# Silu attention: one silu instruction for both units of a group in place of one per unit

## The chip, the cores and the metric

The kernel runs on one core of one Trainium2 chip. The core has a matrix engine (TensorE, PE in the profile; PEld is its loading of weights), a vector engine (VectorE, DVE), an activation engine (ScalarE, ACT), a general engine (GpSimd, POOL) and a queue for transfers (SyncE, SP). Each engine runs its own instructions in the order of the program; between engines semaphores are counted up and waited for. The metric is device time in microseconds (us) of one execution.

## The reference, cut to what matters

Six layers run one after the other on 64 images of 1024 positions and 32 channels. The third is the one that the change touches:

```python
q = silu(x @ Wq + bq); k = silu(x @ Wk + bk); v = silu(x @ Wv + bv); u = x @ Wu + bu
scores = einsum('bhnd,bhmd->bhnm', qh, kh) / sqrt(hd)            # 4 heads of 8
scores = where(causal, scores * scores, 0.0)
self_attn = einsum('bhnm,bhmd->bhnd', silu(scores), vh)
# beside it pos_attn from a table of relative positions, a layer norm, a gate with u, a projection
```

There is no softmax: each score is squared, masked, put through silu, and the weights so made multiply v.

## The kernel before, in words

The layer is `silu_attention_layer`. One image at a time is in the middle of the work; a *stage* of the pipeline (`body`, run for each image by `over_stages`, 12 stages to one turn of a loop) also prepares the two images behind it and finishes the two ahead of it. The attention of an image is cut into 12 groups, `GROUPS_B`: a pair (qc, kb) of one half of the queries and one block of 128 keys. A group has two *units*, one for each pair of heads, so a stage has 24 units, n = 0 to 23. A unit's tile has 128 partitions (keys) and 2 x m columns (two heads, m queries), where m is 512, 384, 256 or 128, by how much of the triangle is left.

A unit goes through these steps:

- PE, `scores` (L890): two matmuls into `p_s[n % 2]`. There are two such tiles, so scores of unit n wait until unit n-2 has been read from its tile.
- The square. For 16 units ACT reads the scores and writes the squares, `square_scores` (L819), into the ring `sq` of 8 units. For the other 8 (`ON_DVE`: n = 0, 1, 6, 7, 12, 13, 18, 19) DVE reads and masks them, `read_scores` (L1037), and POOL squares them in SBUF (L739). Eight of ACT's units lie on the diagonal and are masked afterwards by POOL's `select` (L745).
- ACT, `weigh` (L830): silu of the squares into the ring `wt` of 8 units, `LAG` = 5 units behind the scores.
- PE, `add_up` (L903): for each group, at odd n, the eight matmuls of both units with v into `p_o`; four units further back.

PE's and ACT's orders are written out by hand: for each n, ACT squares unit n (if it is its own) and then weighs unit n-5; PE computes the scores of n, then one piece of the other images' work (`M_PLACE`: transposes of k, q, o; projections; positions; the output L984), then, at odd n, an `add_up`. In what follows S(n) is the scores of unit n on PE, sq(n) the square on ACT, W(n) the silu of unit n. All of them use semaphores: `scored`, `act_squared`, `dve_read`, `weighed` (counted once per unit), `summed` (once per group).

```python
if n >= 2:
    semaphore, value = scores_read(o, n - 2)   # PE: the tile's last reader, ACT or DVE
    pe.wait_ge(semaphore, value)
```

The page of the profile names the tiles with a letter for each layer: `b_` is this one.

Of the kernel before, what the change touches and what calls it, by code (L numbers as in the profile page):

```python
# [8 lines left out]
ACT = mybir.ActivationFunctionType  # L9
# [395 lines left out]
def wait(eng, semaphore, value):  # L405

    if not isinstance(value, int) or value > 0:
        eng.wait_ge(semaphore, value)
# [66 lines left out]
def over_stages(eng, body):  # L475

    for w in range(B_FIRST, B_LOOPED):
        body(Stage(w))
    with eng.Fori(0, (B - 2 - B_LOOPED) // B_UNROLL) as k:
        for d in range(B_UNROLL):  # L480
            body(Stage(B_LOOPED + d, k))
    for w in range(B - 2, B_LAST + 1):
        body(Stage(w))
# [121 lines left out]
def silu_attention_layer(nc, t, kept):  # L605
# [3 lines left out]
    with ExitStack() as ctx:  # L609
        def sb(name, shape, dt=F32):  # L610
            return ctx.enter_context(nc.sbuf_tensor("b_" + name, shape, dt))
# [4 lines left out]
        def sem(name):  # L616
            return ctx.enter_context(nc.semaphore("b_" + name))

        SQ_RING, RING, LAG = 8, 8, 5
# [20 lines left out]
        sq = sb("sq", [P, SQ_RING, 2, HALF])  # L640
        wt = sb("wt", [P, RING, 2, HALF])
# [18 lines left out]
        NG = len(GROUPS_B)  # L660
        UNITS = [(qc, kb, g) for qc, kb in GROUPS_B for g in range(2)]
        N = len(UNITS)
# [4 lines left out]
        def span(n):  # L667

            qc, kb, _ = UNITS[n]
            q0 = max(qc * HALF, kb * P)  # L670
            return q0, (qc + 1) * HALF - q0
# [14 lines left out]
        pool_squared, selected, weighed, summed = (  # L686
            sem("pool_squared"), sem("selected"), sem("weighed"), sem("summed"))
# [18 lines left out]
        @block.sync  # L706
        def _(sp):
            sp.dma_start(x_in[:, 0, :, :], image(src, 0)).then_inc(x_loaded[0], 16)

            def store(i):  # L710
                sp.wait_ge(result_made, i + 1)
                sp.dma_start(image(dst, i), result[:, :, :]).then_inc(stored, 16)

            def body(st):
                if "prep" in st.on:
                    q = st.image("prep")
                    if st.ref > B_FIRST:
                        wait(sp, base_made, q - 1)
                        sp.dma_start(x_in[:, st.place("prep", 2), :, :], image(src, q)).then_inc(x_loaded[st.place("prep", 2)], 16)
                if "past" in st.on:  # L720
                    store(st.image("past"))

            over_stages(sp, body)
            sp.wait_ge(stored, 16 * B)
# [83 lines left out]
        @block.scalar  # L808
        def _(act):
            act.preload_act_table(ACT.Silu)  # L810

            def body(st):
                q, nx, o, p = st.image("prep"), st.image("next"), st.image("own"), st.image("prev")

                def square_scores(n):
                    act.wait_ge(scored, 2 * N * o + 2 * (n + 1))
                    wait(act, weighed, N * o + (n + 1 - SQ_RING))
                    m = span(n)[1]
                    act.activation(sq[:, n % SQ_RING, :, 0:m], p_s[n % 2][:, :, 0:m], ACT.Square).then_inc(act_squared, 1)  # L819

                def weigh(i, n):
                    if n in ON_DVE:
                        act.wait_ge(pool_squared, len(ON_DVE) * i + (ON_DVE.index(n) + 1))
                    elif n in SELECTED:
                        act.wait_ge(selected, len(SELECTED) * i + (SELECTED.index(n) + 1))
                    else:
                        act.wait_ge(act_squared, len(ON_ACT) * i + (ON_ACT.index(n) + 1))
                    wait(act, summed, NG * i + (n // 2 + 1 - RING // 2))
                    m = span(n)[1]
                    act.activation(wt[:, n % RING, :, 0:m], sq[:, n % SQ_RING, :, 0:m], ACT.Silu,  # L830
                                   scale=1.0 / D).then_inc(weighed, 1)

                def silu_qkv(a):
                    act.wait_ge(m_made, st.made(f"qkv{a}"))
                    act.activation(qkv[:, st.place("prep", 2), :, 4 * a:4 * a + 4, :].rearrange("p k r c -> p r k c"),
                                   p_m[st.bank(f"qkv{a}")][:, 0:4 * 3 * C].rearrange("p (r k c) -> p r k c", k=3, c=C),
                                   ACT.Silu).then_inc(qkv_made, 1)

                for n in range(N):
                    if "own" in st.on and n in ON_ACT:  # L840
                        square_scores(n)
                    if "own" in st.on and n >= LAG:
                        weigh(o, n - LAG)
                    if "prev" in st.on and n < LAG:
                        weigh(p, N + n - LAG)
                    if "prep" in st.on and n in (13, 14):
                        silu_qkv(n - 13)

            over_stages(act, body)

        @block.tensor
        def _(pe):
# [5 lines left out]
            def body(st):  # L858
                q, nx, o, p = st.image("prep"), st.image("next"), st.image("own"), st.image("prev")
# [33 lines left out]
                def add_up(i, place, a):  # L893

                    qc, kb = GROUPS_B[a]
                    q0, m = span(2 * a)
                    if a == FIRST_OF[qc]:
                        wait(pe, o_copied, 2 * i - 1 + qc)
                    if a == 0:
                        pe.wait_ge(v_made, i + 1)  # L900
                    pe.wait_ge(weighed, N * i + (2 * a + 2))
                    for h in range(H):
                        ins = pe.matmul(p_o[qc][32 * h:32 * h + 32, q0 - qc * HALF:q0 - qc * HALF + m],  # L903
                                        v_pad[:, place, kb, h, :], wt[:, (2 * a + h // 2) % RING, h % 2, 0:m],
                                        start=(a == FIRST_OF[qc]), stop=(a == LAST_OF[qc]), tile_position=(0, 32 * h),
                                        skip_group_check=True)
                    ins.then_inc(summed, 1)
# [81 lines left out]
                for n in range(N):  # L989
                    if "own" in st.on:  # L990
                        scores(n)
                    for name in M_PLACE.get(n, ()):
                        if name in ("k0", "k1", "q0", "q1") and "next" in st.on:
                            turn_parts(name)
                        elif name in ("o0", "o1") and "prev" in st.on:
                            turn_o(int(name[1]))
                        elif name == "xlT" and "prep" in st.on:
                            turn_xl()
                        elif name in ("qkv0", "qkv1") and "prep" in st.on:
                            project_qkv(int(name[-1]))  # L1000
                        elif name[:3] == "pos" and "next" in st.on:
                            positions(int(name[-1]))
                        elif name == "nT" and "prev" in st.on:
                            turn_normed()
                        elif name == "uT" and "prev" in st.on:
                            project_u()
                        elif name == "out" and "past" in st.on:
                            project_out()
                    if n % 2:
                        a = (n - LAG - 4) // 2  # L1010
                        if a >= 0 and "own" in st.on:
                            add_up(o, st.place("own", 3), a)
                        if a < 0 and "prev" in st.on:
                            add_up(p, st.place("prev", 3), NG + a)
# [4 lines left out]
        def _(dve):  # L1019
# [5 lines left out]
            def body(st):  # L1025
                q, nx, o, p = st.image("prep"), st.image("next"), st.image("own"), st.image("prev")
# [5 lines left out]

                def read_scores(n):
                    dve.wait_ge(scored, 2 * N * o + 2 * (n + 1))
                    wait(dve, weighed, N * o + (n + 1 - SQ_RING))
                    m = span(n)[1]
                    dve.tensor_tensor(sq[:, n % SQ_RING, :, 0:m], p_s[n % 2][:, :, 0:m],  # L1037
                                      tri[:, 0:m].rearrange("p (r m) -> p r m", r=1).broadcast_to([P, 2, m]),
                                      ALU.mult).then_inc(dve_read, 1)
# [105 lines left out]
                for n in range(N):  # L1145
                    if "own" in st.on and n in ON_DVE:
                        read_scores(n)
# [506 lines left out]
RING = 8  # L1654
# [914 lines left out]
```

## Time and profile before

| | |
|---|---|
| time, median of 3 runs | 6068.95 us (6066.87 to 6073.85) |
| span of the profiled execution | 6064.5 us (of that execution nothing beside the span is given; the median is 4.45 us above it) |
| busy over the whole span | PE 89%, DVE 81%, ACT 79%, POOL 52% |
| this layer in steady state (441.31 to 2379.44 us, 60 stages) | PE 1805.26 us, ACT 1760.66, POOL 1476.09, DVE 1353.97 of 1938.13 |
| L830, the silu of this layer | 1440 instructions there, 1162.19 us busy |
| one undisturbed stage | 31.31 to 31.39 us |

A stage's length is read between two starts of the line L1099, which each stage has once on DVE. Busy times count an instruction from its start to its end; on ACT an instruction begins up to 0.1 us before the end of the one ahead, so sums of durations can be above the busy time. In the timeline a row is one instruction or several alike in a row (x2, x8), and the bracket at its end is the engine's idle time just before, with what ended it.

### The profile page before, as it was taken

The page shows a single profiled execution, that of the slowest core. Times are in us where ns is not written, and L with a number is a line of the kernel's source. Part 1 is how long each engine was busy: PE and PEld are TensorE (multiplying, and loading weights), DVE is VectorE, ACT ScalarE, POOL GpSimd, SP SyncE. Part 2 cuts the span into 40 slices and gives each one's busy share as a digit, 9 for nine tenths or more (in the row PEclk, how much of TensorE's full clock was granted, in tenths as well). Part 3 has the DMA queues.
Part 4 walks back from the last instruction along what each step waited for, and adds up shares of the span by engine and source line. Part 5 has one row for each costly group of instructions (what it writes and reads, how often), then busy time and mean ns, then how long its engine had stood idle before and what let it go on. Part 6 is the DMA issues. An engine that isn't in the chain of part 4 may idle for free.

```text
span 6064.5 us, 145558 instructions
## 1 busy us (share of the span) xinstructions
PE 5411.5 (89%) x43064; PEld 2287.0 (38%) x43064; DVE 4920.5 (81%) x9311; ACT 4808.2 (79%) x8146; POOL 3146.1 (52%) x3711
## 2 busy tenths in 40 slices
PE   6679999999999999468999999999999999999997
PEld 5234444444444444352333333333333333333332
DVE  7857667667677676658999999999999999999995
ACT  1159989999899899315888888888888888888887
POOL 1147777777777777632444444444444444444443
PEclk9889999999999999777999999999999999999999
DMA  3010000000000000230000000000000000000000
GB/s 114 22 48 10 9 11 10 9 10 10 9 10 10 9 10 8 63 115 7 9 9 9 9 10 9 9 9 10 10 9 9 10 9 9 9 10 9 9 8 5
DMA packets 400111, 104.64 MB, mean 17 GB/s; under 512 B 348547, under 2 KB 398676, under 8 KB 398804
## 3 DMA queue, kind: packets, MB, share of 16 engines
q1 hardware_dynamic: 398163, 94.72, 7.2%
q8 instruction: 409, 6.70, 0.5%
q14 instruction: 387, 3.16, 0.2%
q10 hardware_dynamic: 1152, 0.05, 0.0%
HBM read 61.17 MB, written 33.56 MB: 16 GB/s over the span
## 4 chain that ended last, share of the span: by engine, by line
PE 25%; DVE 17%; issue 7%; POOL 3%; ACT 2%; DVEq 1%; ACTq 0%; POOLq 0%
DVE d_peaks L2355 13%; PE d_p_o L2193 8%; PE d_p_s L2180 5%; PE d_p_k L2205 4%; PE d_p_s L2293 2%; POOL d_rstd L1989 2%; PE d_p_s L2168 2%; ACT d_wt L2077 2%; PE d_p_s L2251 1%; PE d_p_s L2233 1%; PE d_p_s L2242 1%; DVE d_squares L2373 1%; DVE d_total L2365 1%; POOL d_xl L1993 1%; ACT d_answers L2073 1%
## 5 line engine op out<-in xcount | busy, mean ns | idle before, releaser
L2355 DVE TENSOR_REDUCE d_peaks<-d_p_k 128x1 f32<-128x512 f32 x4096 | 2576.9, 681 | 203.4 <-PE d_p_k L2205 167.9
L2077 ACT ACTIVATE d_wt<-d_p_s 128x512 f32<-128x512 f32 x4096 | 2214.7, 616 | 333.2 <-PE d_p_s L2180 326.7
L2205 PE MATMUL d_p_k<-d_kT,d_qT 64*128 64x512 bf16 x4096 | 1320.6, 387 | 122.4 <-DVE d_peaks L2355 118.9
L2180 PE MATMUL d_p_s<-d_qT,d_kT 64*128 64x512 bf16 x4096 | 1339.7, 384 | 11.3 <-issue 10.8
L830 ACT ACTIVATE b_wt<-b_sq 128x1024 f32<-128x1024 f32 (+3 forms) x1536 | 1240.5, 845 | 10.1 <-issue 10.1
L2193 PE MATMUL d_p_o<-d_wt,d_v_pad 128*32 128x512 f32 x8192 | 1095.3, 607 | 4.5 <-ACT d_o_sb L2082 3.8
L739 POOL TENSOR_TENSOR b_sq<-b_sq 128x1024 f32<-128x1024 f32 (+1 forms) x512 | 849.5, 1680 | 233.6 <-DVE b_sq L1037 233.6
L819 ACT ACTIVATE b_sq<-b_p_s 128x1024 f32<-128x1024 f32 (+2 forms) x1024 | 776.5, 758 | 183.8 <-PE b_p_s L890 177.7
L1037 DVE TENSOR_TENSOR b_sq<-b_p_s,bc_tri 128x1024 f32<-128x1024 f32 (+1 forms) x512 | 551.5, 1088 | 272.8 <-PE b_p_s L890 207.0
L2180 PEld LDWEIGHTS d_p_s<-d_qT,d_kT 64*128 64x128 bf16 x4096 | 330.6, 93 | 1067.7 <-ACT d_wt L2077 782.8
L2032 POOL TENSOR_TENSOR d_answers<-d_answers,d_mix 128x2048 f32<-128x2048 f32 x64 | 233.0, 3641 | 938.5 <-DVE d_mix L2456 938.5
L903 PE MATMUL b_p_o<-b_wt,b_v_pad 128*32 128x512 f32 (+2 forms) x6144 | 672.4, 510 | 1.5 <-ACT b_wt L830 1.0
L890 PE MATMUL b_p_s<-b_qT,b_kT 64*128 64x512 bf16 (+3 forms) x3072 | 503.2, 338 | 144.4 <-DVE b_sq L1037 120.1
L2205 PEld LDWEIGHTS d_p_k<-d_kT,d_qT 64*128 64x128 bf16 x4096 | 322.5, 93 | 427.6 <-DVE d_peaks L2355 360.4
L1982 POOL TENSOR_TENSOR d_square<-d_centred 128x256 f32<-128x256 f32 x128 | 78.3, 612 | 682.0 <-DVE d_centred L2368 682.0
L890 PEld LDWEIGHTS b_p_s<-b_qT,b_kT 64*128 64x128 bf16 x3072 | 137.7, 93 | 749.6 <-issue 262.2
L745 POOL TENSOR_SCALAR_AFFINE_SELECT b_sq<-b_sq 128x256 f32<-128x256 f32 x512 | 285.6, 561 | 207.4 <-ACT b_sq L819 186.0
L956 PE MATMUL b_p_m<-b_qkv,bc_rel 128*128 128x224 f32 (+7 forms) x1920 | 326.1, 312 | 0.0
L956 PEld LDWEIGHTS b_p_m<-b_qkv,bc_rel 128*128 128x128 f32 x1920 | 276.6, 190 | 37.6 <-issue 25.8
L2034 POOL TENSOR_TENSOR d_answers<-d_answers 128x1024 f32<-128x1024 f32 (+2 forms) x192 | 279.2, 1454 | 15.1
L2073 ACT ACTIVATE d_qT<-d_p_s 128x1024 bf16<-128x1024 bf16 x256 | 267.4, 1045 | 19.4 <-PE d_p_s L2261 15.7
L2193 PEld LDWEIGHTS d_p_o<-d_wt,d_v_pad 128*32 128x32 f32 x8192 | 161.4, 108 | 289.1 <-issue 268.6
(293 smaller groups left out, 7536.8 us busy)
## 6 DMA issues: line engine op xcount, KB each, us to landing
c_slots<-t SPq DMA_DIRECT2D x128, 128.0 KB, 2.5
a_xt<-in_x SPq DMA_DIRECT2D x4, 2048.0 KB, 15.1
a_w<-in_L_conv_W SPq DMA_DIRECT2D x64, 128.0 KB, 2.7
t<-a_rows SPq DMA_DIRECT2D x32, 256.0 KB, 2.4
b_x_in<-t SPq DMA_DIRECT2D x64, 128.0 KB, 2.7
t<-b_result SPq DMA_DIRECT2D x64, 128.0 KB, 2.2
t<-c_slots SPq DMA_DIRECT2D x64, 128.0 KB, 1.9
d_x_in<-t SPq DMA_DIRECT2D x64, 128.0 KB, 2.8
```

What stands on the lines that cost most here:

```text
L739: pool.tensor_tensor(at, at, at, ALU.mult).then_inc(pool_squared, 1)
L819: act.activation(sq[:, n % SQ_RING, :, 0:m], p_s[n % 2][:, :, 0:m], ACT.Square).then_inc(act_squared, 1)
L830: act.activation(wt[:, n % RING, :, 0:m], sq[:, n % SQ_RING, :, 0:m], ACT.Silu, scale=1.0 / D).then_inc(weighed, 1)
L890: pe.matmul(p_s[n % 2][:, r, 0:m], kT[rows, u, g, kb * P:(kb + 1) * P], qT[rows, u, g, q0:q0 + m], start=True, stop=True).then_inc(scored, 1)
L903: ins = pe.matmul(p_o[qc][32 * h:32 * h + 32, q0 - qc * HALF:q0 - qc * HALF + m], v_pad[:, place, kb, h, :], wt[:, (2 * a + h // 2) % RING ...
L956: ins = pe.matmul(at[:, n0 * C:(n0 + count) * C], rel[:, x0:x0 + P], v[:, m0:m0 + count, :].rearrange("p j c -> p (j c)"), start=(d == 0), ...
L1037: dve.tensor_tensor(sq[:, n % SQ_RING, :, 0:m], p_s[n % 2][:, :, 0:m], tri[:, 0:m].rearrange("p (r m) -> p r m", r=1).broadcast_to([P, 2, m]),
L2077: act.activation(wt[:, n % RING, :], tile(n)[:, :], ACT.Exp, scale=SCALE).then_inc(s_used, 1)
L2180: pe.matmul(seat(n)[:, :], kT[rows, win.slot("own"), h // 2, kb * P:(kb + 1) * P], qT[rows, win.slot("own"), h // 2, qc * HALF:(qc + 1) * ...
L2193: ins = pe.matmul(p_o[32 * h:32 * h + 32, :], v_pad[:, slot, kb, h, :], wt[:, (H * a + h) % RING, :], start=(kb == 0), stop=(kb == J - 1), ...
L2205: pe.matmul(free_bank((m, r))[:, :], qT[rows, slot, g, j * P:(j + 1) * P], kT[rows, slot, g, half * HALF:(half + 1) * HALF], start=True, s ...
L2355: dve.tensor_reduce(peaks[:, m, r:r + 1], bank((m, r))[:, :], X, ALU.max).then_inc(k_used, 1)
```

## The change

`weigh` is called once per group a, at even n, for units 2a and 2a+1 together: one instruction over both units' slots in the rings, 4 x m columns (up to 2048) in place of two of 2 x m. It comes at the place in ACT's order at which the second of the two units was weighed; the first unit's own instruction, one unit earlier, is gone. It waits for what the second unit waited for. The semaphore `weighed` is now counted once per group (NG = 12 in a stage), so three waits on it are rewritten: ACT's and DVE's for a free slot in the ring `sq` (now the whole group four groups back) and PE's in `add_up` (the same group as before).

```diff
-                    wait(act, weighed, N * o + (n + 1 - SQ_RING))
+                    wait(act, weighed, NG * o + (n // 2 + 1 - SQ_RING // 2))
...
-                def weigh(i, n):
+                def weigh(i, a):
+                    n = 2 * a + 1
...
-                    wait(act, summed, NG * i + (n // 2 + 1 - RING // 2))
+                    wait(act, summed, NG * i + (a + 1 - RING // 2))
                     m = span(n)[1]
-                    act.activation(wt[:, n % RING, :, 0:m], sq[:, n % SQ_RING, :, 0:m], ACT.Silu,
+                    at, of = (2 * a) % RING, (2 * a) % SQ_RING
+                    act.activation(wt[:, at:at + 2, :, 0:m].rearrange("p u r m -> p (u r) m"),
+                                   sq[:, of:of + 2, :, 0:m].rearrange("p u r m -> p (u r) m"), ACT.Silu,
                                    scale=1.0 / D).then_inc(weighed, 1)
...
-                    if "own" in st.on and n >= LAG:
-                        weigh(o, n - LAG)
-                    if "prev" in st.on and n < LAG:
-                        weigh(p, N + n - LAG)
+                    if n % 2 == 0:
+                        a = (n - LAG - 1) // 2
+                        if a >= 0 and "own" in st.on:
+                            weigh(o, a)
+                        if a < 0 and "prev" in st.on:
+                            weigh(p, NG + a)
...
-                    pe.wait_ge(weighed, N * i + (2 * a + 2))
+                    pe.wait_ge(weighed, NG * i + (a + 1))
```

ACT's order from unit 2 of a stage to unit 5, before (`b_p_s0` and `b_p_s1` are the two tiles of scores; L819 is the square, L830 the silu; these are sq(2), W(21) of the image before, sq(3), W(22), sq(4), W(23), sq(5), then W(0) to W(2)):

```order
L819 ACTIVATE b_sq<-b_p_s0 128x1024
L830 ACTIVATE b_wt<-b_sq 128x1024
L819 ACTIVATE b_sq<-b_p_s1 128x1024
L830 ACTIVATE b_wt<-b_sq 128x2x128
L819 ACTIVATE b_sq<-b_p_s0 128x2x256
L830 ACTIVATE b_wt<-b_sq 128x2x128
L819 ACTIVATE b_sq<-b_p_s1 128x2x256
L830 ACTIVATE b_wt<-b_sq 128x1024 x3
```

The same place now (the silu is line L833):

```order
L819 ACTIVATE b_sq<-b_p_s0 128x1024
L833 ACTIVATE b_wt<-b_sq 128x2048
L819 ACTIVATE b_sq<-b_p_s1 128x1024
L819 ACTIVATE b_sq<-b_p_s0 128x2x256
L833 ACTIVATE b_wt<-b_sq 128x4x128
L819 ACTIVATE b_sq<-b_p_s1 128x2x256
L833 ACTIVATE b_wt<-b_sq 128x2048
```

Between sq(2) and sq(3) there now stand both units W(20) and W(21); W(20) stood ahead of sq(2). W(0), which stood behind sq(5) with W(1) and W(2), is in one with W(1), and W(2) has gone behind sq(8).

ACT's order from unit 17 to the start of the next stage, before (sq(17), W(12) and W(13), W(14), sq(20), W(15), sq(21), W(16), sq(22), W(17), sq(23), W(18) and W(19)):

```order
L819 ACTIVATE b_sq<-b_p_s1 128x2x128
L830 ACTIVATE b_wt<-b_sq 128x2x384 x2
L830 ACTIVATE b_wt<-b_sq 128x1024
L819 ACTIVATE b_sq<-b_p_s0 128x1024
L830 ACTIVATE b_wt<-b_sq 128x1024
L819 ACTIVATE b_sq<-b_p_s1 128x1024
L830 ACTIVATE b_wt<-b_sq 128x2x128
L819 ACTIVATE b_sq<-b_p_s0 128x2x128
L830 ACTIVATE b_wt<-b_sq 128x2x128
L819 ACTIVATE b_sq<-b_p_s1 128x2x128
L830 ACTIVATE b_wt<-b_sq 128x2x384 x2
```

The same place now:

```order
L819 ACTIVATE b_sq<-b_p_s1 128x2x128
L833 ACTIVATE b_wt<-b_sq 128x4x384
L819 ACTIVATE b_sq<-b_p_s0 128x1024
L833 ACTIVATE b_wt<-b_sq 128x2048
L819 ACTIVATE b_sq<-b_p_s1 128x1024
L819 ACTIVATE b_sq<-b_p_s0 128x2x128
L833 ACTIVATE b_wt<-b_sq 128x4x128
L819 ACTIVATE b_sq<-b_p_s1 128x2x128
L833 ACTIVATE b_wt<-b_sq 128x4x384
```

Here W(14) has gone from ahead of sq(20) to between sq(20) and sq(21), in one with W(15). The orders of PE, DVE and POOL are as they were.

## Rows read from the trace of the kernel before

**Rows 1.** Page of the profile, first line.

```profile
span 6064.5 us, 145558 instructions
```

**Rows 2.** Busy us by stretch: length, PE, PEld, DVE, ACT, POOL, PE's clock, DMA.

```profile
957.21:988.52 31.31, 29.32 (x244) 14.40 (x244) 22.63 (x39) 29.29 (x43) 24.59 (x26) 1.00 0.06 10
988.52:1021.32 32.80, 30.81 (x244) 15.00 (x244) 22.48 (x39) 29.41 (x43) 24.58 (x26) 0.95 0.06 9
827.67:861.79 34.12, 32.30 (x252) 15.63 (x249) 22.67 (x40) 29.91 (x43) 24.09 (x25) 0.91 0.05 10
...
441.31:2379.44 1938.13, 1805.26 (x14640) 881.49 (x14640) 1353.97 (x2281) 1760.66 (x2521) 1476.09 (x1501) 0.97 0.06 10
```

**Rows 3.** Groups of ACT, 441.31 to 2379.44: count, busy us, mean ns, idle before, releaser.

```profile
L830 ACT ACTIVATE b_wt<-b_sq 128x1024 f32<-128x1024 f32 x720 | 732.7, 1056 | 0.0
L819 ACT ACTIVATE b_sq<-b_p_s 128x1024 f32<-128x1024 f32 x481 | 491.4, 1022 | 129.7 <-PE b_p_s L890 124.8
...
L830 ACT ACTIVATE b_wt<-b_sq 128x256 f32<-128x256 f32 x240 | 100.6, 419 | 0.0
```

**Rows 4.** Timeline of ACT, stage 1505.83 to 1537.22: start, duration, line, idle before.

```profile
1505.36 1.02 ACT L819 ACTIVATE b_sq<-b_p_s 128x1024 f32<-128x1024 f32 x1 [0.24 <-PE b_p_s L890]
1506.28 1.05 ACT L830 ACTIVATE b_wt<-b_sq 128x1024 f32<-128x1024 f32 x1
1507.22 1.02 ACT L819 ACTIVATE b_sq<-b_p_s 128x1024 f32<-128x1024 f32 x1
...
1509.69 2.96 ACT L830 ACTIVATE b_wt<-b_sq 128x1024 f32<-128x1024 f32 x3
1512.60 1.02 ACT L819 ACTIVATE b_sq<-b_p_s 128x1024 f32<-128x1024 f32 x1
...
1514.47 1.02 ACT L819 ACTIVATE b_sq<-b_p_s 128x1024 f32<-128x1024 f32 x1
...
1523.28 1.03 ACT L819 ACTIVATE b_sq<-b_p_s 128x1024 f32<-128x1024 f32 x1
...
1530.06 1.02 ACT L819 ACTIVATE b_sq<-b_p_s 128x1024 f32<-128x1024 f32 x1 [1.45 <-PE b_p_s L890]
1530.98 1.05 ACT L830 ACTIVATE b_wt<-b_sq 128x1024 f32<-128x1024 f32 x1
1531.93 1.01 ACT L819 ACTIVATE b_sq<-b_p_s 128x1024 f32<-128x1024 f32 x1
```

**Rows 5.** Timeline of PE, the same stage.

```profile
1507.92 0.62 PE L915 MATMUL b_p_m<-bc_ident,b_parts 128*128 128x128 bf16 x8
1508.48 0.28 PE L890 MATMUL b_p_s<-b_qT,b_kT 64*128 64x256 bf16 x2
...
1510.24 0.60 PE L890 MATMUL b_p_s<-b_qT,b_kT 64*128 64x512 bf16 x4
...
1512.07 0.39 PE L890 MATMUL b_p_s<-b_qT,b_kT 64*128 64x512 bf16 x2 [0.28 <-DVE b_sq L1037]
1513.80 0.39 PE L890 MATMUL b_p_s<-b_qT,b_kT 64*128 64x512 bf16 x2 [1.34 <-DVE b_sq L1037]
...
1516.46 0.28 PE L890 MATMUL b_p_s<-b_qT,b_kT 64*128 64x256 bf16 x2
...
1525.44 0.23 PE L890 MATMUL b_p_s<-b_qT,b_kT 64*128 64x128 bf16 x2
...
1532.75 0.48 PE L890 MATMUL b_p_s<-b_qT,b_kT 64*128 64x128 bf16 x4
```

**Rows 6.** Timeline of PE's weight loads, 1532.5 to 1533.3 us.

```profile
1532.99 0.10 PEld L890 LDWEIGHTS b_p_s<-b_qT,b_kT 64*128 64x128 bf16 x2 [0.15 <-ACT b_sq L819]
```

**Rows 7.** Timeline of DVE, the same stage.

```profile
1510.79 1.22 DVE L1037 TENSOR_TENSOR b_sq<-b_p_s,bc_tri 128x1024 f32<-128x1024 f32 x1 [0.82 <-ACT b_wt L830]
```

**Rows 8.** Timeline of PE, one add_up in the stage from 957.21, one from 988.52.

```profile
965.96 1.06 PE L903 MATMUL b_p_o<-b_wt,b_v_pad 128*32 128x512 f32 x8
...
997.27 1.57 PE L903 MATMUL b_p_o<-b_wt,b_v_pad 128*32 128x512 f32 x8
```

More of the change, by code:

```diff
@@ L1034, in read_scores @@
                     dve.wait_ge(scored, 2 * N * o + 2 * (n + 1))
-                    wait(dve, weighed, N * o + (n + 1 - SQ_RING))
+                    wait(dve, weighed, NG * o + (n // 2 + 1 - SQ_RING // 2))
                     m = span(n)[1]
```

## Prediction

> **What bounds the kernel now.** The change touches one layer, so I read the busy time by stretch first, the groups of ACT second, the timelines of one stage last. The profiled execution spans 6064.5 us [rows 1]; the median of the runs shown is 6068.95, so 4.45 us lie around the span, and they are added at the end. Sixty whole stages of the layer take 1938.13 us. In an undisturbed stage of 31.31 us PE is busy 29.32 and ACT 29.29, so by the shares either could be the bound, and both are idle for 2.0 us [rows 2]. The groups of ACT tell them apart. The silu (L830) has no idle time ahead of it, while the squares of 1024 columns wait 129.7 us, 124.8 of it for PE's scores [rows 3]. ACT is full but follows. In the timelines PE runs through its list and stands still longest at S(8) and S(9), 0.28 and 1.34 us, both for DVE's reading of the scores [rows 5]. That pair of waits starts with S(6): the row at 1510.24 holds S(6) and S(7), S(6) is done at about 1510.24 + 0.39 (the duration of a single one in the row of S(8)) = 1510.63, and DVE reads it at 1510.79 [rows 5, 7]. The row puts DVE's 0.82 us of idle time down to ACT's silu; but DVE needs S(6) first, and it begins 0.16 after that is done, so it follows PE. So a stage is PE's own list plus what DVE and ACT make it wait, and ACT counts only where a square comes too late for a tile of scores.
>
> **The gain on ACT.** A silu of 1024 columns takes 1056 ns, one of 256 takes 419 [rows 3]: 637 over 768 columns, 0.83 ns a column, 0.85 us for 1024. Three in a row take 2.96 us from first start to last end [rows 4]; less one duration of 1.06 that is 1.90 for two steps, 0.95 each. The fixed part of a step is 0.95 - 0.85 = 0.10 us. A merged silu of 2048 columns then holds ACT for 0.95 + 0.85 = 1.80 us in place of 1.90 and lasts about 1.06 + 0.85 = 1.91. Twelve instructions fewer in a stage give 1.2 us of ACT's time; over some 62 full stages (64 images less filling and draining) 74 us. ACT already has 2.0 us to spare in each stage [rows 2], so I count this gain at nothing.
>
> **What moves, and where it lands.** Half of the silus now stand between two squares between which only one stood. Which square is late, and does PE feel it? There are two tiles of scores, so S(n) needs the square or reading of n-2.
>
> - sq(3) and S(5). sq(2) starts at 1505.36 when PE has its scores (0.24 us idle, for PE), W(21) at 1506.28, sq(3) at 1507.22 [rows 4]. Now W(20) and W(21) together follow sq(2): sq(3) starts at 1506.28 + 1.80 = 1508.08 and ends at 1509.10. From the end of sq(21), 1531.93 + 1.01 = 1532.94, to PE's load at 1532.99 are 0.05 us [rows 4, 6]. S(5) would start at 1509.15. It started at 1508.48, behind the transposes that began at 1507.92, without a wait [rows 5]. Cost 0.67 us. That W(20) no longer stands ahead of sq(2) gives nothing back, since sq(2) waits for PE.
> - sq(21) and S(23). sq(20) waits 1.45 us for PE, W(15) starts at 1530.98, sq(21) at 1531.93 [rows 4]; the scores of unit 23 are the second half of the row at 1532.75 and their weights are loaded at 1532.99, released by sq(21) [rows 5, 6]. There is no slack at all. With W(14) and W(15) in one, sq(21) comes 1.80 - 0.95 = 0.85 later. Cost 0.85 us.
> - sq(9) and S(11). sq(8) starts at 1512.60, W(2) and W(3) in one follow 0.92 later (the step of a square, 1505.36 to 1506.28), sq(9) at 1515.32 in place of 1514.47, done at 1516.34; PE would get it at 1516.39, and S(11) starts at 1516.46 [rows 4, 5]. Hidden, with 0.07 us left. If that cover is gone, 0.1 to 0.2.
> - sq(15) and S(17). sq(15) ends at 1523.28 + 1.03 = 1524.31, now 0.85 later at 1525.16; S(17) starts at 1525.44 [rows 4, 5]. Hidden. The second silu of q, k and v lies between and is late by as much; DVE's next steps on it feed the next image, a stage away.
>
> Behind S(5) and S(23) PE has everything else in its queue, the add_ups among it, and DVE's readings of units 6, 7, 0 and 1 begin when PE's scores arrive, so the delays are passed on whole: 0.67 + 0.85 = 1.52 us a stage, 62 stages, **94 us**. The rewritten waits of DVE and ACT for a slot in the ring look four groups back, to silus that stand ahead of them in ACT's order by two units or more; add_up waits for the same group as before, whose merged silu ends about 0.1 us sooner than the pair did where nothing else holds it. I cost these at nothing.
>
> **The clock.** The stage from 988.52 is 32.80 long and not 31.31, and PE's granted clock in it is 0.95, so for a part of it PE ran at the lower of its two levels, 1.2 GHz [rows 2]. Its add_up right behind the wait before S(9) took 1.57 us where its twin of the stage before took 1.06 [rows 8]. One such fall costs 32.80 - 31.31 = 1.49 us. By the starts of L1099, 35 of the sixty stages are of the short kind and 17 of the long; eight stand at turns of the loop, where PE waits more, and the one from 827.67 has 0.91 and 34.12 us [rows 2]. The wait before S(9) stays, and PE's idle time in a stage rises from 2.0 to 3.5 us, so I expect more stages with a fall. How many can't be read from any row. The ends are none more (0 us) and all 35 short ones (35 x 1.49 = 52 us); fewer falls, 17 x 1.49 = 25 us given back, have no reason with more idle time. The nearest rows with more idle time are the turns of the loop, which have their falls, so I go near the upper end: 45 us.
>
> **The sum.** 6064.5 + 94 + 45 = 6203.5 us of span; with 4.45 around it 6208.
>
> **A rule of the Trainium skill.** ACT idles 2.0 us of a stage, mostly waiting for scores [rows 2, 3]. The Trainium skill, Trace Analysis, section Optimizing Scalar/DVE Operations, puts some 93 ns of fixed engine time on each ScalarE instruction on SBUF, advises grouping where the engine is saturated, and breaking instructions up where it isn't but causes bubbles elsewhere. The trace agrees with the price (0.10 us) and puts this kernel under the second half. By the first half alone the estimate would be 744 x 0.093 = 69 us faster, by the second the time gets longer.
>
> **The rivals.**
>
> - ACT is the bound after all: faster. Then each stage loses the fixed parts of twelve instructions, 1.2 us, and 62 stages 74 us: 5995. For it speaks that ACT is as busy as PE, 29.29 of 31.31 us [rows 2]. Against it stand the 124.8 us for scores [rows 3]. It decides if PE's waits before S(5) and S(23) don't come.
> - The delays come, the falls of the clock stay as frequent: 6064.5 + 94 + 4.45 = 6163. For it: the two new waits are each shorter than the one before S(9), after which the clock fell. Against it: more idle time in the same stage.
> - Only one delay arrives. If PE is held before S(5) or S(23) for something else anyway, 0.67 x 62 = 42 or 0.85 x 62 = 53 us remain: 6111 or 6122.
> - Nothing arrives, because PE comes to both places later than the rows show or DVE's chain from unit 6 to S(9) doesn't begin with S(6) and takes up the rest: 6069. Against it: no slack at S(23) [rows 6].
>
> **How the numbers follow.** Delays with more falls, 6208 (its own range 6180 to 6235): 0.48. Delays without more falls, 6163: 0.27. One delay, 6111 to 6122: 0.10. No change: 0.07. Faster, 5995: 0.08. What a measurement of this kernel can tell from no change is about 0.2%, 12 us; so faster 0.08, same 0.07, slower 0.85. The low end of the range is one delay without more falls, 6111, taken as 6110. The high end takes 94 + 52, 12 us more if the cover at S(11) fails by 0.2 in 62 stages, and a second fall in one stage of three (20 x 1.49 = 30): 188, or 6257, taken as 6260.
>
> **What would show it.** Right: 768 silus (12 for each of 64 images) with means near 1.91 us at 2048 columns; PE idle about 0.67 us before S(5) and 0.85 before S(23), released by ACT's square L819; a stage near 32.8 us at full clock and 34.3 with a fall; ACT's idle time in a stage at 4 to 5 us, for PE; the wait before S(9) still about 1.34. The prediction is wrong if a stage at full clock is shorter than 32 us, or PE waits in other places, or a silu of 2048 columns isn't near 1.91. If only the clock differs, the mean of PEclk over the layer tells by how much.

## The result, and the profile after

The changed kernel takes 6213.9 us (median of 4 runs, 6205.4 to 6216.87), 1.0239 times the kernel before (95% interval 1.0226 to 1.0251): slower by about 146 us. Forecast were 6208, between 6110 and 6260.

Busy time by stretch, first two plain stages, then sixty stages, as in [rows 2] (length, then busy us of PE, PEld, DVE, ACT, POOL, PE's granted clock, DMA share, GB/s):

```profile
1554.02:1588.15 34.13, 30.83 (x245) 14.71 (x244) 22.39 (x39) 28.12 (x31) 24.11 (x26) 0.95 0.05 9
1588.15:1622.28 34.13, 30.82 (x245) 14.72 (x244) 22.39 (x39) 28.12 (x31) 24.11 (x26) 0.95 0.05 9
446.76:2523.41 2076.65, 1863.47 (x14641) 891.77 (x14640) 1343.96 (x2282) 1688.43 (x1801) 1451.20 (x1501) 0.94 0.05 9
```

The sixty stages take 2076.65 us where they took 1938.13 [rows 2]: 138.5 of the 150.6 us by which the span grew (6215.1 against 6064.5). The profiled execution of the changed kernel is the longest of its four (6216.87). ACT works 1.17 us less in a stage, 28.12 against 29.29, and the stage is 2.8 us longer. All 52 plain stages (those that don't stand at a turn of the loop) now look like the long ones of before, at a granted clock of 0.95. A *fall* is such a stretch at the lower of PE's two clocks.

The groups of ACT over the sixty stages (count, busy us, mean ns, idle time just before, its releaser), against [rows 3]:

```profile
L833 ACT ACTIVATE b_wt<-b_sq 128x2048 f32<-128x2048 f32 x360 | 687.1, 1909 | 0.0
L819 ACT ACTIVATE b_sq<-b_p_s 128x1024 f32<-128x1024 f32 x481 | 491.0, 1021 | 325.7 <-PE b_p_s L896 325.7
```

The merged silu lasts 1909 ns, no more than its columns and one fixed part. The squares wait 325.7 us for PE's scores, where they waited 124.8: ACT follows more than it did.

PE in the stage from 1554.02 (start, duration, line, idle time before and what ended it), against [rows 5]. The waits are those of S(5), S(8), S(9) and S(23):

```profile
1557.42 0.28 PE L896 MATMUL b_p_s<-b_qT,b_kT 64*128 64x256 bf16 x2 [0.69 <-ACT b_sq L819]
...
1560.93 0.39 PE L896 MATMUL b_p_s<-b_qT,b_kT 64*128 64x512 bf16 x2 [0.19 <-DVE b_sq L1043]
1562.66 0.46 PE L896 MATMUL b_p_s<-b_qT,b_kT 64*128 64x512 bf16 x2 [1.34 <-DVE b_sq L1043]
...
1563.68 1.94 PE L909 MATMUL b_p_o<-b_wt,b_v_pad 128*32 128x512 f32 x8
...
1566.63 0.28 PE L896 MATMUL b_p_s<-b_qT,b_kT 64*128 64x256 bf16 x2
...
1584.02 0.23 PE L896 MATMUL b_p_s<-b_qT,b_kT 64*128 64x128 bf16 x2 [0.87 <-ACT b_sq L819]
```

S(5) had no wait and now has 0.69 us, S(23) has 0.87, both for ACT's square; S(11), at 1566.63, has none. S(8) waits 0.19, and S(3), which waited 0.21 for DVE before, has no marked wait any more. The wait before S(9) is 1.34 as before, and the add_up behind it takes 1.94 us, where its twins of before took 1.06 at full clock and 1.57 with a fall [rows 8].

ACT in the same stage, against [rows 4]: sq(2), the merged silu, and a row of two that begins with sq(3); then the merged silu ahead of sq(21), and a row of two that begins with sq(21):

```profile
1553.63 1.02 ACT L819 ACTIVATE b_sq<-b_p_s 128x1024 f32<-128x1024 f32 x1 [1.37 <-PE b_p_s L896]
1554.55 1.90 ACT L833 ACTIVATE b_wt<-b_sq 128x2048 f32<-128x2048 f32 x1
1556.36 1.50 ACT L819 ACTIVATE b_sq<-b_p_s 128x1024 f32<-128x1024 f32 x2
...
1580.22 1.02 ACT L819 ACTIVATE b_sq<-b_p_s 128x1024 f32<-128x1024 f32 x1 [2.04 <-PE b_p_s L896]
1581.14 1.90 ACT L833 ACTIVATE b_wt<-b_sq 128x2048 f32<-128x2048 f32 x1
1582.94 1.29 ACT L819 ACTIVATE b_sq<-b_p_s 128x1024 f32<-128x1024 f32 x2
```

sq(3) starts 1.81 us behind the silu ahead of it, 0.94 before. In front of sq(2) and sq(20) ACT now stands idle 1.37 and 2.04 us, where it stood 0.24 and 1.45: W(20) and W(14) used to fill part of that time, and they have been moved behind the square, where PE waits for what comes after them.

### The profile page after: what moved, and what is told of

Read it like the earlier page. It is cut to its first block, busy times and chain, and to the rows that moved or that the text cites. A ratio compares the mean times of both kernels' runs of the same rounds, so it can differ in the third digit from the quotient of the medians.

```text
span 6215.1 us, 143541 instructions
## 1 busy us (share of the span) xinstructions
PE 5476.0 (88%) x43064; PEld 2297.5 (37%) x43064; DVE 4911.4 (79%) x9311; ACT 4732.4 (76%) x7378; POOL 3120.3 (50%) x3711
## 4 chain that ended last, share of the span: by engine, by line
PE 25%; DVE 16%; issue 7%; POOL 3%; ACT 2%; DVEq 1%; ACTq 0%; POOLq 0%
DVE d_peaks L2361 12%; PE d_p_o L2199 7%; PE d_p_s L2186 5%; PE d_p_k L2211 4%; PE d_p_s L2299 2%; POOL d_rstd L1995 2%; PE d_p_s L2174 1%; ACT d_wt L2083 1%; PE d_p_s L2257 1%; PE d_p_s L2239 1%; PE d_p_s L2248 1%; DVE d_squares L2379 1%; DVE d_total L2371 1%; POOL d_xl L1999 1%; ACT d_answers L2079 1%
## 5 line engine op out<-in xcount | busy, mean ns | idle before, releaser
L833 ACT ACTIVATE b_wt<-b_sq 128x2048 f32<-128x2048 f32 (+3 forms) x768 | 1143.6, 1489 | 13.8 <-issue 13.8
L819 ACT ACTIVATE b_sq<-b_p_s 128x1024 f32<-128x1024 f32 (+2 forms) x1024 | 755.1, 758 | 403.4 <-PE b_p_s L896 402.7
L909 PE MATMUL b_p_o<-b_wt,b_v_pad 128*32 128x512 f32 (+2 forms) x6144 | 711.0, 537 | 1.0 <-ACT b_wt L833 0.9
L745 POOL TENSOR_SCALAR_AFFINE_SELECT b_sq<-b_sq 128x256 f32<-128x256 f32 x512 | 255.8, 500 | 392.4 <-ACT b_sq L819 375.7
```

Of the source, the lines that this page charges most:

```text
L833: act.activation(wt[:, at:at + 2, :, 0:m].rearrange("p u r m -> p (u r) m"), sq[:, of:of + 2, :, 0:m].rearrange("p u r m -> p (u r) m"), A ...
```

## The experiments

The theory was that two merged silus stand ahead of a square that PE needs at once, and that PE's clock falls follow its wait before S(9), oftener as the stage is longer. Stage lengths are read between starts of the result's line on DVE. Of the sixty stages 52 are plain and eight stand at turns of the loop. Each count of falls is that of one execution, the profiled one. In the ratios the kernel before is that of the same round, 6066.58 us for the first four experiments and 6073.4 for the last three.

**Two groups apart (split_7_10).** Groups 7 and 10 as before, the other ten merged:

```diff
+                APART = (7, 10,)
...
+                    if part is not None:
+                        ins = act.activation(wt[:, n % RING, :, 0:m], sq[:, n % SQ_RING, :, 0:m], ACT.Silu, scale=1.0 / D)
+                        if part:
+                            ins.then_inc(weighed, 1)
+                        return
```

> Ten of the twelve groups keep the merged silu; groups 7 and 10 (units 14, 15 and 20, 21), whose merged silus stand ahead of sq(21) and sq(3), go back to two instructions in the places of before. Theory (the cost is two squares that come too late for PE): PE's waits before S(5) and S(23), 0.69 and 0.87 us in the changed kernel, go, a stage at full clock is 31.3 us again, the clock falls in about one stage of three, 6068 us within 15. Rival 1 (each merged silu costs, wherever it stands): ten twelfths of the loss stay, about 6190. Rival 2 (the falls of the clock in every stage have nothing to do with those two waits): 94 us go, the rest stays, about 6120.

6054.39 us, 0.9981 of before (0.9971 to 0.999). Both waits are gone. The only waits of PE that its timeline marks in the plain stage from 1338.00 are these two, before S(8) and S(9), and the stage is 31.26 long at full clock:

```profile
1344.15 0.39 PE L901 MATMUL b_p_s<-b_qT,b_kT 64*128 64x512 bf16 x2 [0.19 <-DVE b_sq L1048]
1345.88 0.39 PE L901 MATMUL b_p_s<-b_qT,b_kT 64*128 64x512 bf16 x2 [1.34 <-DVE b_sq L1048]
```

```profile
1338.00:1369.26 31.26, 29.39 (x245) 14.44 (x244) 22.61 (x39) 28.30 (x33) 23.98 (x26) 1.00 0.06 10
1400.53:1433.14 32.61, 30.81 (x245) 15.00 (x244) 22.38 (x39) 28.41 (x33) 24.33 (x26) 0.95 0.06 10
```

13 of 52 plain stages are of the long kind, 17 before. So two groups of twelve hold the whole loss; rivals 1 and 2 are out. The clock's part went with the two waits.

**Two instructions at the new place (two_in_place).**

```diff
-                    at, of = (2 * a) % RING, (2 * a) % SQ_RING
-                    act.activation(wt[:, at:at + 2, :, 0:m].rearrange("p u r m -> p (u r) m"),
-                                   sq[:, of:of + 2, :, 0:m].rearrange("p u r m -> p (u r) m"), ACT.Silu,
-                                   scale=1.0 / D).then_inc(weighed, 1)
+                    for u in (2 * a, 2 * a + 1):
+                        ins = act.activation(wt[:, u % RING, :, 0:m], sq[:, u % SQ_RING, :, 0:m], ACT.Silu, scale=1.0 / D)
+                    ins.then_inc(weighed, 1)
```

> The two silus of a group are two instructions again, one right behind the other, at the place of the merged one and counted once per group. Theory (the place costs, not the merging): as slow as the changed kernel or a little slower, since two steps take 1.90 us in place of 1.80, so the waits before S(5) and S(23) grow by about 0.1 each and one of about 0.1 may come before S(11): 6214 to 6235. Rival (a silu of 2048 columns itself costs, by a late signal or a slower pass): back to 6068.

6198.49 us, 1.0222 of before (1.0205 to 1.0239). The rival is out: the loss belongs to the place, with or without the merging. The waits grew by 0.1 as worked out; the rows are S(5), S(8), S(9) and S(23):

```profile
1514.81 0.28 PE L895 MATMUL b_p_s<-b_qT,b_kT 64*128 64x256 bf16 x2 [0.78 <-ACT b_sq L819]
1518.31 0.39 PE L895 MATMUL b_p_s<-b_qT,b_kT 64*128 64x512 bf16 x2 [0.19 <-DVE b_sq L1042]
1520.04 0.39 PE L895 MATMUL b_p_s<-b_qT,b_kT 64*128 64x512 bf16 x2 [1.34 <-DVE b_sq L1042]
1540.33 0.23 PE L895 MATMUL b_p_s<-b_qT,b_kT 64*128 64x128 bf16 x2 [0.96 <-ACT b_sq L819]
```

The time is nevertheless below the range expected, 6214 to 6235. The clock fell in 41 of 52 plain stages and not in all, 33.16 us without a fall and 34.46 with one:

```profile
1374.83:1407.99 33.16, 29.51 (x245) 14.42 (x244) 22.65 (x40) 29.12 (x43) 23.93 (x26) 1.00 0.05 9
1442.53:1476.99 34.46, 30.92 (x245) 14.80 (x244) 22.38 (x40) 29.23 (x43) 24.12 (x26) 0.95 0.05 9
```

That only makes up for the longer stages: the 52 plain stages take 1775.9 us together, 1777.4 in the changed kernel. The 14.3 us by which the sixty stages are shorter (2062.33 against 2076.65) lie in the eight at turns of the loop, 286.4 against 299.3. The second stage of the third turn shows it, the changed kernel's first; the granted clock is higher:

```profile
1696.38:1731.40 35.02, 32.51 (x252) 15.79 (x250) 22.57 (x40) 28.62 (x31) 23.48 (x25) 0.91 0.05 9
```

```profile
1685.10:1718.70 33.60, 30.88 (x252) 15.35 (x250) 22.63 (x40) 29.50 (x43) 23.63 (x25) 0.97 0.05 9
```

**The merged silu behind the odd square (odd).**

```diff
-                    if n % 2 == 0:
-                        a = (n - LAG - 1) // 2
+                    if n % 2:
+                        a = (n - LAG) // 2
```

> The merged silu of each group stands one unit earlier in ACT's order, behind the square of the odd unit in place of the even one, so sq of an even unit and the sq behind it stay next to each other and the long silu comes after both. Theory: sq(3) and sq(21) come in time, PE waits before S(5) and S(23) go; since ACT's saved time is off the path, no faster than before: 6068 within 15, ACT's idle time near 3.2 us a stage. Rival 1 (any silu of 1.9 us delays some square that PE needs, now the even ones: S(10), S(12), S(22)): above 6150. Rival 2 (ACT's saved time counts once the order is right): about 5995.

6031.33 us, 0.9944 of before (0.9928 to 0.9961): faster, and neither of the figures expected. ACT's busy time is 28.39 in a plain stage and ACT idles 2.8 there (3.2 over the sixty, as expected). The plain stage below is 31.15 long, 0.16 less than the 31.31 of before, which is all that a stage at full clock gives:

```profile
1360.32:1391.47 31.15, 29.18 (x245) 14.34 (x244) 22.75 (x39) 28.39 (x32) 24.69 (x26) 1.00 0.06 10
1422.64:1455.10 32.46, 30.63 (x245) 14.92 (x244) 23.10 (x39) 28.74 (x32) 24.39 (x26) 0.95 0.06 10
```

The waits before S(5) and S(23) are gone, and no square is waited for. The marked waits of that stage are those before S(8) and S(9) and a new one of 0.18 us, before matmuls on the positions, for ACT's silu of q, k and v:

```profile
1366.47 0.39 PE L896 MATMUL b_p_s<-b_qT,b_kT 64*128 64x512 bf16 x2 [0.19 <-DVE b_sq L1043]
1368.20 0.39 PE L896 MATMUL b_p_s<-b_qT,b_kT 64*128 64x512 bf16 x2 [1.34 <-DVE b_sq L1043]
...
1375.85 1.75 PE L962 MATMUL b_p_m<-b_qkv,bc_rel 128*128 128x256 f32 x8 [0.18 <-ACT b_qkv L839]
```

Over the sixty stages it gains 37.1 us (1901.01 against 1938.13): 17.2 in the eight stages at turns of the loop (265.3 against 282.5 together) and 20 in the 52 plain ones, where 11 are long in place of 17. Rival 1 is out, and so is rival 2 as it was put: half of the 74 us comes back, and most of that not from a shorter stage at full clock. At the turns the granted clock is higher: 1.00 in the last four of the eight stages, where before none had more than 0.98. What makes it higher stays open.

**DVE's copy of q1 behind its reading of unit 7 (after_q1).** In the changed kernel:

```diff
-                        if n == 6:
+                        if n == 7:
                             copy_parts("q1")
```

> The changed kernel with one step of DVE moved: the copy of q1 stands behind its reading of unit 7 in place of ahead of it. DVE's copy takes 0.59 us of the chain S(6), read(6), copy, read(7), S(9), so the wait before S(9) falls from 1.34 to about 0.75; the waits before S(5) and S(23) stay. Theory (the falls of the clock come from the wait before S(9)): the falls go too, a stage is 34.13 - 0.59 - 1.26 = 32.28 us, 62 stages give back 115 us: about 6100. Rival 1 (the falls come with the longer stage or with the new waits): 0.59 x 62 = 37 us back, 6177, a fall in every stage still. Rival 2 (another wait takes the place of this one): 6214.

6130.65 us, 1.0109 of before (1.0093 to 1.0126), 83 below the changed kernel. The wait before S(9) fell to 0.74 as expected, but 0.60 came back in two new waits, for the copy (the transposes of xl) and for sq(9) (S(11)), so the time is above the 6100 expected:

```profile
1514.46 0.39 PE L896 MATMUL b_p_s<-b_qT,b_kT 64*128 64x512 bf16 x2 [0.74 <-DVE b_sq L1043]
1515.14 0.41 PE L937 MATMUL b_p_m<-bc_ident,b_xl 128*128 128x128 f32 x2 [0.30 <-DVE b_qT L1068]
...
1517.65 0.28 PE L896 MATMUL b_p_s<-b_qT,b_kT 64*128 64x256 bf16 x2 [0.30 <-ACT b_sq L819]
```

And the falls are gone from all 52 plain stages, each 32.88 us at full clock:

```profile
1506.41:1539.29 32.88, 29.51 (x245) 14.42 (x244) 22.62 (x39) 28.02 (x31) 24.43 (x26) 1.00 0.05 9
```

At full clock this stage is as long as the changed kernel's would be by its waits, 31.31 + 0.69 + 0.87 = 32.87, and PE idles 3.4 us in it; what differs is that the wait of 1.34 is split into shorter ones. So the falls hang on the 1.34 us wait before S(9) and not on the idle time of the stage. By the same figures 34.13 - 32.88 = 1.25 us is what a fall costs in the changed kernel. Rival 1 is out (there the falls stay), and rival 2 holds for the 0.60 alone.

**One group apart (split_10).** As the first, with `APART = (10,)`.

> Eleven groups keep the merged silu; only group 10 (units 20 and 21, ahead of sq(3)) is two instructions in the places of before. Theory (the two waits are separate and add up): the wait before S(5) goes, the one of 0.87 before S(23) stays, a stage at full clock is 32.88 - 0.69 = 32.2 us, as 31.27 + 0.87 = 32.1 says from the other side. Without falls of the clock in more stages than before that is 6054 + 60 x 0.87 = 6106, with a fall in every stage about 6165. Rival (one wait hides the other, as each lets ACT catch up): 6054 or 6214.

6145.14 us, 1.0122 of before (1.0105 to 1.0139). The wait for S(23) stands at 0.87, that for S(5) is gone, and a stage at full clock is 32.12: the two add up. The clock falls in 35 of 52 plain stages, between the two ends expected. The first row is the wait in a plain stage at full clock, then come that stage and one with a fall:

```profile
1343.45 0.23 PE L901 MATMUL b_p_s<-b_qT,b_kT 64*128 64x128 bf16 x2 [0.87 <-ACT b_sq L819]
```

```profile
1315.46:1347.58 32.12, 29.41 (x245) 14.43 (x244) 22.59 (x39) 28.10 (x32) 23.97 (x26) 1.00 0.06 10
1381.10:1414.57 33.47, 30.81 (x245) 14.99 (x244) 22.39 (x40) 28.21 (x32) 24.36 (x26) 0.95 0.06 10
```

**The copy of q1 moved, in the kernel before (before_q1).** The same edit.

> The kernel before with DVE's copy of q1 behind its reading of unit 7. Theory: the wait before S(9) falls from 1.34 to 0.74 as in the changed kernel with this step, the transposes of xl behind S(9) wait 0.30 for the copy, so a stage at full clock goes from 31.3 to 31.0; and the falls of the clock, which followed the wait of 1.34, go from plain stages. 60 x 0.3 = 18 and 17 x 1.49 = 25 us: about 6024. Rival (the falls stay, one in three stages): 6049.

6020.69 us, 0.9918 of before (0.9901 to 0.9934). PE's wait before S(9) is now 0.74, the transposes of xl wait 0.30, and the 0.21 and 0.28 before S(3) and S(8) are as before; a plain stage is 30.97, and 3 of 52 are long. As expected.

```profile
1360.78 0.39 PE L890 MATMUL b_p_s<-b_qT,b_kT 64*128 64x512 bf16 x2 [0.74 <-DVE b_sq L1037]
1361.46 0.41 PE L931 MATMUL b_p_m<-bc_ident,b_xl 128*128 128x128 f32 x2 [0.30 <-DVE b_qT L1062]
```

```profile
1353.40:1384.37 30.97, 29.32 (x244) 14.41 (x244) 22.57 (x40) 29.07 (x43) 24.66 (x26) 1.00 0.06 10
```

**Both (odd_q1).** The merged silu behind the odd square and the copy of q1 behind unit 7.

> The merged silu behind the odd square, and DVE's copy of q1 behind its reading of unit 7. Theory: as above, from the 6031 of the merged silu in that place: 0.3 us less in each stage (18 us) and no falls of the clock in plain stages (11 falls of about 1.3, 14 us): about 6000. Rival 1 (ACT has sq(9) late, as in the changed kernel with this step, and the wait comes back before S(11)): 6015 or above. Rival 2 (no gain beside the falls): 6017.

5995.62 us, 0.9876 of before (0.986 to 0.9893): faster than both kernels. No plain stage has a fall, and PE waits for no square of ACT, so rivals 1 and 2 are out:

```profile
1342.81:1373.63 30.82, 29.19 (x245) 14.34 (x244) 22.69 (x40) 28.31 (x32) 24.73 (x26) 1.00 0.06 10
```

## Why the prediction was right

- **ACT is not the bound.** Right. 1.17 us less work in a stage (1.2 forecast) bought nothing; the squares' wait for scores grew. The odd place gives the nearest thing to ACT's saving without the two waits, and a stage at full clock is 0.16 us shorter there, not 1.2.
- **S(5) and S(23).** Right in place, releaser and size: 0.69 and 0.87 measured, 0.67 and 0.85 forecast. split_7_10 shows that these two groups are all of the loss, split_10 that the two waits add up, two_in_place that it is the place of the silu and not its length as one instruction.
- **S(11) and S(17).** Hidden, as forecast. In the changed kernel's plain stages the fall just ahead of S(11) delays it anyway; that it is hidden at full clock is shown by split_7_10, where units 2 and 3 are merged too and nothing is marked there. How thin the cover of 0.07 us at S(11) is shows in after_q1: with S(9) 0.6 us earlier the wait there appears, 0.30.
- **The sum of the waits.** The stage at full clock, which the changed kernel never shows, is taken from 31.31 + 0.69 + 0.87 = 32.87 (after_q1, where 0.60 of one wait became two of 0.30, has 32.88). That it comes out so well has two small terms in it that cancel: the waits before S(3) and S(8) shrank by 0.09 us each (the one before S(3) to an unmarked 0.12), and PE's busy time at full clock is 0.19 more (29.51 in after_q1 against 29.32). 1.56 us in 60 stages are 94 us; filling and draining and the rest of the span hold the other 12 of the 150.6 us, for which the forecast, which charged 62 stages, had allowed 3. The 4.45 us that it put around the span are not that: in the changed kernel's profiled execution 1.8 us lie there (6216.87 against 6215.1), and the rest is taken to be the distance of the profiled execution of before from the median. The forecast of the difference doesn't use them.
- **The clock.** 138.5 - 94 = 45 us remain over the sixty stages, and 45 was forecast. That the two agree is in part luck. The falls come in every plain stage and not in nearly every one, and each costs 1.25 us and not 1.49. In the 52 plain stages that is 52 x 1.25 - 17 x 1.49 = 40 us; the other 5 lie at the turns. The direction was argued from more idle time on PE, and that reason doesn't hold by itself: after_q1 has the two new waits and PE idle for 3.4 us of a stage, about the 3.5 of the forecast, and no fall, since the old wait of 1.34 is cut.
- **What would show it.** A stage with a fall is 34.13 (34.3 forecast). ACT's idle time in a stage is 34.13 - 28.12 = 6.0 us; 4 to 5 was said, which fits a stage without a fall (32.88 - 28.02 = 4.9 in after_q1).
- **The rivals.** Faster, with ACT as the bound, and no change are out. The delays without more falls, 6163, are out by the 52 falls in place of 17. One delay alone is what split_10 has, at 6145 and not at 6111 to 6122, because its falls were more, too.
- **The rule of the Trainium skill** (Perfetto Trace Analysis, section Optimizing Scalar/DVE Operations) pointed the right way in its second half: where ScalarE isn't saturated but causes bubbles on other engines, breaking instructions up may help. The runs agree on the bubbles, 0.69 and 0.87 us on PE, but not that breaking up suffices: two_in_place has two instructions again and waits of 0.78 and 0.96. What counts here is which square stands behind the silus: the same merged silu one unit earlier in the order leaves no wait before S(5) and S(23), and one of 0.18 elsewhere.

## What to carry to other kernels

A longer instruction on an engine that isn't the bound costs what the next instruction in its queue is late, so look at who waits for that one and how much slack it has; two places of twelve held the whole loss here. Merging also moves one of the two pieces, and the work that filled a wait may land behind the instruction that ended it. So put the merged piece behind the work that another engine needs at once, not ahead of it.

## What was not expected of the hardware

How often the lower clock was granted, with the same wait of 1.34 us before S(9), followed no simple measure of PE's waits. Of 52 plain stages 11 had a fall at a stage of 31.2 us (odd), 13 at 31.3 (split_7_10), 17 at 31.3 (before), 35 at 32.1 (split_10), 41 at 33.2 (two_in_place) and 52 where a stage would be 32.9 (after). Executions of one kernel differ, too: the four of the kernel before beside the result go from 6056.02 to 6073.85 us, which would be a dozen falls at 1.49, so 11, 13 and 17 can't be told apart by one execution each. But 41 against 52 speaks against any rule by the length of the stage or by the sum of the waits: two_in_place has the longer stage and 0.18 us more of waiting before S(5) and S(23), and over the whole program a mean granted clock of 0.953 to 0.957 in its four executions, where the changed kernel has 0.950 to 0.952. What sets the number stays open; that a wait of 0.74 in place of 1.34 takes it to 0 or 3 was shown in three kernels.
